# A fused attention and gated-recurrence kernel: the query product of tiles 3 to 7 in three fp32r passes, and the key bias of tiles 2 and 3 copied by ScalarE

## What is computed

```
Q = x @ Wq.T + bq ; K = x @ Wk.T + bk ; V = x @ Wv.T + bv
Q = elu(Q) + 1 ; K = elu(K) + 1
KV = einsum('bnd,bne->bde', K, V)
Z  = einsum('bnd,bd->bn', Q, K.sum(axis=1) + 1e-6)
x  = layernorm(x + (einsum('bnd,bde->bne', Q, KV) / Z) @ Wo.T + bo)

# FFN: a recurrence over the first axis of x (8 steps here)
for xt in steps:                      # gated recurrence
    f = sigmoid(xt @ wf.T + c @ uf.T + bf)
    i = sigmoid(xt @ wi.T + c @ ui.T + bi)
    g = tanh(xt @ wc.T + c @ uc.T + bc)
    c = f * c + i * g
h = tanh(x @ wo.T + c_final @ uo.T + bo)
x = layernorm(x + h)
```

## Time and profile before

| | us |
|---|---|
| median of 3 runs | 103.72 (103.26 to 103.76) |
| the profiled execution | 102.75 |
| its span in the trace | 101.0 |
| PE busy | 91.6 (91%) |
| PEld busy (weight loads, beside PE) | 78.8 (78%) |
| DVE busy | 80.9 (80%) |
| ACT busy | 68.5 (68%) |
| POOL busy | 42.1 (42%) |

### The profile page before, as it was taken

One profiled execution on the slowest core, in us unless ns is written; L12 is line 12 of the kernel. 1 busy time (PEld: TensorE's weight loads), 2 busy tenths in 40 slices (PEclk: granted clock), 3 DMA queues, 4 the chain that ended last, 5 costly groups with the idle time before them and its releaser, 6 DMA issues.

```text
span 101.0 us, 1930 instructions
## 1 busy us (share of the span) xinstructions
PE 91.6 (91%) x607; PEld 78.8 (78%) x607; DVE 80.9 (80%) x234; ACT 68.5 (68%) x143; POOL 42.1 (42%) x65
## 2 busy tenths in 40 slices
PE   5989999999799999999999999999999999896700
PEld 4859879688488978978888999989899999785300
DVE  3256598979999996898689989996455999999970
ACT  1465767587497694785869445599365949889760
POOL 2004598148358058019306704260500055455870
PEclk9999999999999999999999999999999999999998
DMA  1869999100000000000000000000000000153366
GB/s 37 295 210 295 401 394 368 46 0 3 0 0 0 0 0 0 10 0 0 0 0 0 6 0 0 0 3 3 6 0 0 0 0 0 47 168 104 104 208 208
DMA packets 5413, 7.36 MB, mean 73 GB/s; under 512 B 507, under 2 KB 3228, under 8 KB 5404
## 3 DMA queue, kind: packets, MB, share of 16 engines
q1 hardware_dynamic: 4972, 6.92, 19.4%
q10 hardware_dynamic: 432, 0.33, 1.2%
HBM read 5.15 MB, written 2.10 MB: 72 GB/s over the span
## 4 chain that ended last, share of the span: by engine, by line
PE 57%; DVE 27%; issue 5%; ACT 4%; POOL 3%; DVEq 0%; POOLq 0%; ACTq 0%
PE ps_ctx L433 7%; PE ps_k L410 6%; PE ps_q L424 6%; PE ps_ctx L453 5%; DVE stats L1140 5%; PE ps_f L397 4%; DVE x L1129 3%; DVE x L960 3%; PE ps_x L467 2%; DVE s L1011 2%; DVE x L975 2%; DVE x L1156 2%; DVE new L1004 2%; PE ps_ctx L443 2%; PE ps_f L481 2%
## 5 line engine op out<-in xcount | busy, mean ns | idle before, releaser
L346 POOL TENSOR_TENSOR s_lo<-s,s_hi 128x512 fp32r<-128x512 f32 (+1 forms) x8 | 8.1, 1012 | 24.6 <-ACT s_hi L752 24.6
L333 POOL TENSOR_TENSOR rstd<-var_eps,minus_half 128x4 f32<-128x4 f32 (+1 forms) x9 | 9.1, 1010 | 12.6 <-DVE var_eps L1148 12.6
L317 POOL TENSOR_TENSOR rstd<-var_eps,minus_half 128x4 f32<-128x4 f32 x8 | 8.6, 1078 | 6.6 <-DVE var_eps L951 6.5
L308 POOL TENSOR_TENSOR k_pair<-k_rows 128x256 f32<-128x256 f32 x8 | 6.3, 782 | 9.1 <-DVE k_rows L986 9.1
L960 DVE TENSOR_SCALAR x<-x,stats,rstd 128x128 f32<-128x128 f32 x26 | 10.0, 441 | 0.0
L805 ACT ACTIVATE x_hi<-ps_x 128x512 fp32r<-128x512 f32 x8 | 4.8, 594 | 6.2 <-PE ps_x L467 6.2
L736 ACT ACTIVATE th_f<-ps_f,half_b 128x256 f32<-128x256 f32 (+1 forms) x11 | 5.8, 530 | 4.4 <-PE ps_f L513 4.3
L410 PE MATMUL ps_k<-wkq,x_cols 128*128 128x128 f32 x64 | 8.5, 276 | 0.0
L722 ACT ACTIVATE k_exp<-ps_k,minus_one 128x512 f32<-128x512 f32 x8 | 5.5, 686 | 4.4 <-PE ps_k L418 3.5
L424 PE MATMUL ps_q<-x_cols,wkq 128*128 128x512 f32 x16 | 8.2, 593 | 0.0
L410 PEld LDWEIGHTS ps_k<-wkq,x_cols 128*128 128x128 f32 x64 | 8.0, 194 | 0.2
(11 more groups left out here) (191 smaller groups left out, 286.6 us busy)
## 6 DMA issues: line engine op xcount, KB each, us to landing
x_cols<-xt SPq DMA_DIRECT2D x8, 256.0 KB, 7.0
x_rows<-x SPq DMA_DIRECT2D x8, 256.0 KB, 7.0
out<-x SPq DMA_DIRECT2D x7, 256.0 KB, 2.2
wgate<-w_gate SPq DMA_DIRECT2D x1, 384.0 KB, 6.6
out<-x SPq DMA_DIRECT2D x2, 128.0 KB, 2.0
wkq<-w_kq ACTq DMA_DIRECT2D x1, 131.0 KB, 3.3
wvo_in<-w_vo_in ACTq DMA_DIRECT2D x1, 128.0 KB, 3.3
wout<-w_out SPq DMA_DIRECT2D x1, 128.0 KB, 6.7
```

The lines of the kernel that those rows point to most:

```text
L308: nc.gpsimd.tensor_tensor(k_pair[:], k_rows[:, a % 2, 0:C // 2], k_rows[:, a % 2, C // 2:C], ALU.add).then_inc(k_pair_ok, 1)
L317: nc.gpsimd.tensor_tensor(rstd[:, b], var_eps[:, b], minus_half[:], ALU.pow).then_inc(rstd_ok, 1)
L333: nc.gpsimd.tensor_tensor(part_of(rstd, u, T), part_of(var_eps, u, T), minus_half[:, 0:nt * H].rearrange("p (t c) -> p t c", c=H), ALU.pow ...
L346: nc.gpsimd.tensor_tensor(s_lo[:, t % 2, part], state(t)[:, part], s_hi[:, t % 2, part].bitcast(F32), ALU.subtract).then_inc(slo_ok[k], 1)
```

## The change

The key bias of tiles 2 and 3 comes by ScalarE's copy, as that of tiles 4 to 7 did. So GpSimd makes `bk_wide` ahead of `halve_weights`, and ScalarE has a `key_bias` in periods 0 and 1 as well.

The query product of tiles 3 to 7 is three fp32r passes: Wq and x are each split in a high part, rounded by a ScalarE copy (`wq_hi`, `xq_hi`), and the rest, by a GpSimd subtraction (`wq_lo`, `xq_lo`). The parts of x of tile k+1 are made in period k-1, behind `input_tanh` on ScalarE and behind `key_sums` on GpSimd, and are double-buffered.

```
-BIAS_BY_PE = 4
+BIAS_BY_PE = 2
+QUERY_FP32 = 3
...
+            def weight_low():
+                pool.wait_ge(wq_hi_ok, 1)
+                nc.gpsimd.tensor_tensor(wq_lo[:], wkq[:, WQ_T * D:(WQ_T + 1) * D], wq_hi[:].bitcast(F32),
+                                        ALU.subtract).then_inc(wq_lo_ok, 1)
+
+            def query_low(a):
+                pool.wait_ge(xq_hi_ok, a - QUERY_FP32 + 1)
+                if a >= QUERY_FP32 + 2:
+                    pool.wait_ge(q_mm, a - 1)
+                nc.gpsimd.tensor_tensor(xq_lo[:, a % 2], x_cols[:, a].rearrange("p c d -> p (c d)"),
+                                        xq_hi[:, a % 2].bitcast(F32), ALU.subtract).then_inc(xq_lo_ok, 1)
...
                 if a == 0:
+                    key_bias()
                     halve_weights()
-                    key_bias()
+                    weight_low()
+                if k + 1 >= QUERY_FP32:
+                    query_low(k + 1)
                 if a == 2:
                     split_state_low()
...
+                if a >= QUERY_FP32:
+                    if a == QUERY_FP32:
+                        pe.wait_ge(wq_lo_ok, 1)
+                    pe.wait_ge(xq_hi_ok, a - QUERY_FP32 + 1)
+                    nc.tensor.matmul(ps_q[:], wq_hi[:], xq_hi[:, a % 2], start=True, stop=False)
+                    nc.tensor.matmul(ps_q[:], wq_lo[:], xq_hi[:, a % 2], start=False, stop=False)
+                    pe.wait_ge(xq_lo_ok, a - QUERY_FP32 + 1)
+                    nc.tensor.matmul(ps_q[:], wq_hi[:], xq_lo[:, a % 2], start=False, stop=True).then_inc(q_mm, 1)
+                    return
...
+            def query_high(a):
+                act.wait_ge(x_cols_in[a], 16)
+                if a >= QUERY_FP32 + 2:
+                    act.wait_ge(q_mm, a - 1)
+                nc.scalar.activation(xq_hi[:, a % 2], x_cols[:, a].rearrange("p c d -> p (c d)"),
+                                     ACT.Copy).then_inc(xq_hi_ok, 1)
...
+            nc.scalar.activation(wq_hi[:], wkq[:, WQ_T * D:(WQ_T + 1) * D], ACT.Copy).then_inc(wq_hi_ok, 1)
...
+                if a <= 1:
+                    key_bias(k + 1)
                 if a > 2:
                     xk_copy(a)
                 if t is not None:
                     forget_tanh(t)
                     key_bias(k + 1)
                     input_tanh(t)
+                if k + 1 >= QUERY_FP32:
+                    query_high(k + 1)
                 if b is not None:
                     x1_high(b)
```

More of the change, by code:

```diff
@@ L130, in build @@
         k_rows = sb("k_rows", [D, 2, C, D])
+        wq_hi = sb("wq_hi", [D, D], F32R)
+        wq_lo = sb("wq_lo", [D, D], F32R)
+        xq_hi = sb("xq_hi", [D, 2, N], F32R)
+        xq_lo = sb("xq_lo", [D, 2, N], F32R)
         q_exp = sb("q_exp", [D, 2, N])
@@ L183, in build @@
         q_mm, q_exp_ok, q_relu_ok, q_ok = sem("q_mm"), sem("q_exp_ok"), sem("q_relu_ok"), sem("q_ok")
+        wq_hi_ok, wq_lo_ok, xq_hi_ok, xq_lo_ok = sem("wq_hi_ok"), sem("wq_lo_ok"), sem("xq_hi_ok"), sem("xq_lo_ok")
         k_pair_ok, k_sum_ok, xk_mm, xk_ok = sem("k_pair_ok"), sem("k_sum_ok"), sem("xk_mm"), sem("xk_ok")
```

## The result

The changed kernel takes 107.80 us in the median of four runs (107.43 to 108.94), against 103.49 for the kernel before in the same comparison: 1.044 times as long, 95% interval 1.035 to 1.054. The profiled execution took 108.94 us, with a span of 107.2 against 101.0.

What follows compares the result with a forecast made beforehand. TensorE's chain, 57%, was taken to bound the kernel, with VectorE at 27%. Terms 2.1 + 0.9 + 0.3 + 0.8 = +4.1 us on the 101.0 span gave 105.1, 106.85 as an execution and 107.8 us as median; range 105.2 to 109.0.

Steps and rivals of the forecast that it cites:

- step 1: Key bias of tile 2: TensorE stands still 1.75 us for ScalarE's copy, saves 0.23; +1.5 us.
- step 3: Query parts of tile 3: third pass waits for `xq_lo`; net -0.1 to +0.3, taken as +0.1; shift +2.1 us.
- step 4: Tile 4: what tile 1's normalisings give back is lost at the third pass; shift stays +2.1 us (1.8 to 2.2).
- step 2: Key bias of tile 3: wait 0.7 us (0.5 to 0.8) for ScalarE's copy, saved 0.23; shift becomes +2.0.
- step 5: State of tile 0: `s` waits for `wgate_lo`, `x_lo` of tile 1 comes late, TensorE waits 0.7 to 1.2; +0.9 us.
- step 7: Into the tail: `xq_lo` of tile 7 pushes `s` of tile 3 back by 1.0; +0.8 us (0.2 to 1.2).
- rival (c): TensorE's stops lower its clock: half for 3 us would add 1.5 us, giving 109.3 us; chance 0.08.
- step 6: Tiles 5 to 7: `xq_lo` pushes `s` back by 1.0; per tile -0.16 + 0.25, together +0.3 us (-0.5 to +1.0).
- the exclusion: `keep`, `new`, `s` on VectorE and `xq_lo` on GpSimd can't run together: the later waits; `s` back by 1.0 us.
- (b): Bias copies of tiles 2 and 3 come in time, `bk_wide` ready by 11.3: -1.9, 101.8 us; chance 0.03.
- (a): Late bias copies cost as forecast, VectorE and GpSimd contention little, `new` and `s` ahead of `wgate_lo`: +1.3, 105.0 us; chance 0.13.
- (d): A pass costs more than 0.23 us: at 0.3 each +0.9 on the sum, 108.7 us; no separate chance given.

Runs made afterwards that it cites:

- The changed kernel with the filling: The changed kernel plus eight fp32r matmuls of ones (1.8 us) into a free bank ahead of the keys of tile 2: 107.90 us, ratio 1.040.
- The early copy: The kernel before with only tile 2's key bias by ScalarE, `bk_wide` made ahead of the key sums of tile 1: 103.65 us, ratio 1.001.
- bias part alone: The kernel before with key bias of tiles 2 and 3 by ScalarE, queries one fp32 product: 106.81 us, ratio 1.030; repeated 107.24 us, ratio 1.033.
- The kernel with writes only: The changed kernel with GpSimd's `xq_lo` subtraction replaced by three memsets of 128x512, low part left out of the result: 107.64 us, ratio 1.039.
- the moved parts: Against the kernel before: queries of tiles 4 to 7 in three passes, parts of x made one period earlier, bias unchanged: 102.90 us, ratio 0.9945.

## Why the prediction held, and where it didn't

The median was forecast to the tenth, 107.8 us, but that owes something to errors that cancel: in the table below steps 1, 3 and 4 were put 1.3 us too low together, steps 2, 5 and 7 1.4 too high. Where TensorE stands, after against before, by the starts of the same instruction in the two timelines:

| | before | after | late by | this step | forecast |
|---|---|---|---|---|---|
| keys_x of tile 0 | 7.48 | 7.95 | 0.47 | 0.47 (start) | - |
| 1: keys_x of tile 1 | 12.95 | 15.25 | 2.30 | 1.83 | 1.5 |
| context of tile 1 | 15.82 | 19.71 | 3.89 | 1.59 (clock) | rival (c) |
| 2: transposes of tile 0 | 17.91 | 22.16 | 4.25 | 0.36 | 0.5 |
| 3: first gate pass of tile 0 | 19.29 | 24.07 | 4.78 | 0.53 | 0.1 |
| 4: first gate pass of tile 1 | 27.13 | 32.49 | 5.36 | 0.58 | 0 |
| 5: keys_x of tile 3 | 29.30 | 34.59 | 5.29 | -0.07 | 0.9 |
| 6: second gate pass of tile 4 | 53.16 | 58.82 | 5.66 | 0.37 | 0.3 |
| 7: first s of the tail | 59.47 | 65.66 | 6.19 | 0.53 | 0.8 |

From there to the end both take the same time. Without start and clock the steps sum to 4.1 us, the forecast's 4.1. The changed kernel with the filling gives the same sum in an execution without the slow stretch: at the places of the table it is late by 1.13, 2.98, 2.90, 3.60, 3.77, 4.35, 4.30, 4.67 and 5.20 us, 4.07 without its start.

**Step 1** held in mechanism, in the engine that is last (GpSimd's `bk_wide`, 12.96 to 13.51, then the copy at 13.54) and in size: a stop of 1.89 against 1.75.

```profile
12.96 0.55 POOL L348 TENSOR_SCALAR bk_wide<-bk_wide 128x128 f32<-128x128 f32 x1
13.54 0.60 ACT L836 ACTIVATE ps_k<-bk_wide 128x512 f32<-128x512 f32 x1 [0.32 <-POOL bk_wide L348]
```

The 0.3 beyond the forecast is that and a slower first group of matmuls behind a stop, which I had not priced. The early copy shows that the order was the cause; that this earlier order gains nothing either was not in the forecast.

**Step 2** held: 0.69 of wait with the clock full (bias part alone, and the changed kernel with the filling), within the 0.5 to 0.8. In the changed kernel's profile it is 0.34; I put that down to the slow stretch ahead, in which ScalarE fell less behind. The group behind this stop is slower too, so that steps 1 and 2 come to 2.5 with the clock full, against 2.0.

**Step 3** looks too small in the table and held with the clock full. There (the changed kernel with the filling) `xq_lo` took 1.65 us, 0.35 more than the 1.30 of the earlier trace rows, as much as was given to the exclusion at most; the third pass waited 0.17, and the step is +0.17 for +0.1. In the profile of the changed kernel `xq_lo` took 1.79, since `q_cols` of tile 2 had started at 21.85, just ahead of it, and the pass waited 0.52: what the shorter wait of step 2 had given comes back here. Steps 2 and 3 together are 0.89 in one and 0.87 in the other.

**Steps 4 and 5** are wrong one by one and right together up to 0.4. The order in which the two engines get their turn was not as I put it. `new` was asked for at 30.30, later than `xq_lo` at 30.08, and still went first, right behind `keep`; so `xq_lo` ended at 32.09, not 0.6 us earlier, and the third pass waited 1.30. In return `s`, waiting since 31.07, went ahead of `wgate_lo` (1.46 instead of 1.00), and `x_lo` came in time for its pass. So the forecast's sign for step 5, a matmul released by `x_lo` near 31.9, did not show. The forecast let each waiting GpSimd instruction go before VectorE's next. In these rows the one that had waited while the other held on went next, and VectorE's next instruction had its turn against a GpSimd instruction that had only just been issued; but with `keep` and `new` VectorE went twice running. The kernel with the filling shows the same order and nearly the same lengths (`xq_lo` 2.03, `s` 1.57, `wgate_lo` 1.47). From a few rows I make no rule of that.

**Steps 6 and 7** held: `s` 1.58 in tiles 1 to 3, the third passes late by 0.2, the wait of `kvo` down to 0.34 from 1.10, and the tail 0.5 later. One size in step 6 was too large: the normalisings took 1.25 us, 0.15 longer, not 0.5. The kernel with writes only shows that the late `s` is the exclusion, and the moved parts show that it comes and goes with the place. The added high ends of the forecast are 5.6 by the bounds that it names, not 5.8.

**The exclusion itself**, the ground of steps 4 to 7, was read off rows of other instructions and held. The Trainium skill, SBUF — State Buffer, section "Who interferes with whom", adds that a GpSimd instruction which only writes does not contend with a VectorE instruction with two SBUF inputs. The kernel with writes only agrees: `s` at 0.69 with memsets all through it.

**Rivals.** (b) fell at once: `bk_wide` was not ready at 11.3. (a) had the order right at tile 0, where `new` and `s` went ahead of `wgate_lo` and step 5 was nothing. It fell all the same: what the normalisings gave back was lost at a third pass that waited 1.30, and VectorE's free time did not take up the rest, 0.5 in the tail. (d) fell: a pass adds 0.23. (c), with a chance of 0.08, is what was underrated. I argued from slices late in the kernel where TensorE waits often and the clock stays up, and gave it 1.5 us if it happened; the very last slice of that row is in fact an 8. It happened in the profiled execution, at 1.6 us, and in the other kernels with that stop in 7 of 14 executions by the mean clock. The argument compared many short waits with one long one; that this was its error is likely, not shown. That the median is still met is luck in part: only one of the four executions here had a mean clock under 0.98.

## What to carry to other kernels

Work on an idle engine is free only beside the right neighbours: before moving fp32 work to GpSimd, look at what VectorE does at that moment, put it beside instructions that read PSUM, and place it early enough that nobody waits for its result (here such subtractions, one per tile, cost 2.4 us in one place, 1.0 of it by their neighbours, and nothing that the runs could show a period earlier and beside readers of PSUM). A copy that takes the place of a matmul pass has to be ready before the pass would have run, and what it waits for on its own engine sets that, not its 0.6 us. And a new stop of TensorE of nearly 2 us can be followed by a slow stretch that costs nearly as much again, 1.6 us here, in some executions; look for it before comparing medians of few runs.

## What the runs showed of the hardware

- A stop of TensorE of 1.9 us was followed, after it had run again for 1.5 us, by 3.1 us at a granted clock of 0.50, in which an fp32 product of 512 columns took 1.91 instead of 1.02 us. It came in 8 of 18 executions by the mean clock, and in none of 10 in which matmuls of ones filled the stop. Whether the filling or the late start of the filled executions kept it away, and why it comes in some executions and not in others, the runs don't show.
- The start also differs between executions of one kernel: in the bias part alone, profiled twice, the keys of tile 0 took 1.91 and 1.05 us, and keys_x of tile 0 started at 8.60 and 7.88. The granted clock is shown as 1.00 over both. Such a difference can move a median of four, whatever the change.
- GpSimd's memset of 128x512 took about 0.5 us beside a VectorE instruction with two SBUF inputs, and neither slowed the other; its subtraction of the same size took 1.3 and held the other up for 0.9. In tile 0 two memsets took 1.24 instead of 0.99 us. They had begun while VectorE's `keep` ran, a TENSOR_SCALAR there with one large input; that `keep` caused it is not shown.
- A group of eight matmuls behind a stop of TensorE took 0.96 to 0.97 us until the next could follow, against 0.81 in an unbroken row.
